# A perceiver block on one core: cross-attention's head in another order, loops written out, the context's split on another engine, and a later turn in the FFN

## The reference

```
x = x + cross_attention(layernorm(x), context)   # 16 heads of 16, 256 keys, Wq, Wk, Wv, Wo of 256 x 256, no mask
x = x + self_attention(layernorm(x))             # 16 heads of 64, causal, 64 queries
x = x + ffn(layernorm(x))                        # 256 -> 1024 -> 256, gelu; x and the hidden layer rounded to
                                                 # 16 bits by their largest magnitude, the weights to 8 bits
```

## Time and profile before

| | |
|---|---|
| the profiled execution's own time | 651.54 us |
| its span, first to last instruction | 649.7 us |
| mean granted clock of TensorE | 0.989 |
| TensorE, matmul / weight load | 602.3 us (93%) / 515.6 us (79%) |
| VectorE | 470.7 us (72%) |
| ScalarE | 386.3 us (59%) |
| GpSimd | 155.4 us (24%) |

### The profile page before, as it was taken

How to read it: one execution, slowest core, us unless ns; L and a number is a source line. 1 busy time by engine, 2 the same in 40 slices (tenths; PEclk the granted TensorE clock), 3 DMA queues, 4 the chain that set the end, 5 groups by cost and what they waited for, 6 DMA issues and landing times. The chain is left out here.

```text
span 649.7 us, 18558 instructions
## 1 busy us (share of the span) xinstructions
PE 602.3 (93%) x6777; PEld 515.6 (79%) x6777; DVE 470.7 (72%) x989; ACT 386.3 (59%) x1016; POOL 155.4 (24%) x219
## 2 busy tenths in 40 slices
PE   6599999999999999889889999999999998699997
PEld 3598888888888898758777979797979797444597
DVE  4478788888888888667899665757575657367797
ACT  3488788888888888755333333333333334257795
POOL 6524243424343423000301212112121203060000
PEclk9799999999999999999999999999999999999999
DMA  6996767676777767804000000000000000000012
GB/s 202 266 259 174 188 158 183 169 191 169 183 175 182 174 163 204 256 15 130 3 2 2 2 0 0 0 0 0 0 0 0 3 2 2 10 0 2 0 49 82
DMA packets 37036, 58.43 MB, mean 90 GB/s; under 512 B 6912, under 2 KB 15232, under 8 KB 36992
## 3 DMA queue, kind: packets, MB, share of 16 engines
q1 hardware_dynamic: 29328, 42.75, 25.7%
q10 hardware_dynamic: 4592, 8.78, 4.7%
q0 software_dynamic: 3072, 6.30, 4.0%
HBM read 17.96 MB, written 2.10 MB: 31 GB/s over the span
## 5 line engine op out<-in xcount | busy, mean ns | idle before, releaser
L617 ACT ACTIVATE Pr<-pS,nmax 128x256 f32<-128x256 f32 x256 | 120.0, 484 | 26.9 <-DVE nmax L725 26.8
L725 DVE TENSOR_REDUCE nmax<-pS 128x2 f32<-128x512 f32 x128 | 87.3, 684 | 21.7 <-PE pS L461 20.1
L471 PE MATMUL pT<-ident,Pr 128*128 128x128 f32 x512 | 78.6, 276 | 3.2 <-DVE wraw L730 3.1
L953 POOL TENSOR_TENSOR a_Pr<-a_Pr,a_rinv 128x512 f32<-128x512 f32 x32 | 32.8, 1045 | 185.8 <-DVE a_rinv L1242 185.8
L461 PE MATMUL pS<-Kst,Qst 96*128 96x256 f32 x256 | 58.9, 313 | 12.4 <-DMA Qst<-QSl 6.9
L1122 ACT ACTIVATE a_Pr<-a_Pr 128x512 f32<-128x512 f32 x32 | 20.2, 631 | 76.0 <-DVE a_Pr L1234 76.0
L471 PEld LDWEIGHTS pT<-ident,Pr 128*128 128x128 f32 x512 | 60.0, 142 | 4.5 <-issue 4.2
L461 PEld LDWEIGHTS pS<-Kst,Qst 96*128 96x128 f32 x256 | 40.3, 194 | 21.1 <-issue 9.1
L617 ACT ACTIVATION_READ_ACCUMULATOR Pr<-pS,nmax 128x1 f32 x256 | 55.1, 215 | 0.0
L280 POOL DMA_DIRECT2D Qst<-QSh x60 | 30.2, 506 | 80.8 <-PE pS L461 56.2
L59 PE MATMUL a_pJ<-a_XTh,a_W1h 128*128 128x256 f32 x128 | 37.1, 290 | 2.5 <-DVE X L1255 1.6
(11 more groups left out here) (316 smaller groups left out, 1972.9 us busy)
## 6 DMA issues: line engine op xcount, KB each, us to landing
Kst<-WO_ints SPq DMA_DIRECT2D x96, 128.0 KB, 3.3
CT<-ctxT ACTq DMA_DIRECT2D x16, 512.0 KB, 4.9
Kst<-KSh SPq DMA_DIRECT2D x62, 128.0 KB, 2.7
Qst<-QSh SPq DMA_DIRECT2D x64, 64.0 KB, 2.4
Qst<-QSh POOLq DMA_DIRECT2D x64, 64.0 KB, 3.0
Kst<-KSl SPq DMA_DIRECT2D x31, 128.0 KB, 3.2
Qst<-QSl SPq DMA_DIRECT2D x32, 64.0 KB, 2.3
Qst<-QSl POOLq DMA_DIRECT2D x32, 64.0 KB, 2.9
```

Source lines behind the costliest of these rows:

```text
L471: last = pe.transpose(pT[s % 2][:, t, k, :], Pr[s % 2][:, t, P * k:P * k + P], ident[:, :])
L617: act.activation(Pr[c % 2][:, t, :], pS[c % 2][:, t, :], ACT.Exp, bias=nmax[c % 2][:, t:t + 1], accum_out=rsum[par][:, c // 4, 2 * (c % 4) ...
L725: dve.tensor_reduce(nmax[s % 2][:, :], pS[s % 2][:, :, :], AX.X, ALU.max, negate=True).then_inc(maxed, 1)
L953: pool.tensor_tensor(rows, rows, rinv[s][:, :].unsqueeze(2).to_broadcast([P, 8, SQ]), ALU.mult).then_inc(weighted, 1)
```

## The change

**Loops.** Cross-attention and self-attention no longer have a loop: all 8 quads are written out, and the waits are by names (`made`) instead of by running numbers with a register in them.

**Events.** V of the next quad's even pair is made at steps 10 and 11 (before: 10 and 14), K of its odd pair at steps 12 and 14 (before: 11 and 12). Quad 0 has no event at steps 6 and 7.

**Head.** The order is K, X, K, Q, V, V of pair 0, K, K of pair 1, and then V, V of pair 1. The matmuls that filled TensorE's wait ahead of Q are gone. x is loaded ahead of the first weights. Of the first K, SP restacks two groups, ScalarE one and GpSimd one. Of the first Q, SP restacks one group, ScalarE one and GpSimd two, the high parts ahead of the low ones in each. On VectorE the low part of pair 1's context comes behind Q.

**Context and norm.** GpSimd now makes the high part of the context as well as the low part, and `normalize` from quad 1 on. ScalarE has the loads only, VectorE the statistics.

**FFN.** The turn stands behind slice 3 (before: 1), the split of the turned x behind slice 4 (before: 2).

The diff, cut:

```diff
-        AHEAD = [("K", 0, 0), ("K", 0, 1), ("X", 0, 0), ("Q", 0, 0), ("V", 0, 0), ("V", 0, 1), ("K", 1, 0), ("K", 1, 1)]
...
+        AHEAD = [("K", 0, 0), ("X", 0, 0), ("K", 0, 1), ("Q", 0, 0), ("V", 0, 0), ("V", 0, 1), ("K", 1, 0), ("K", 1, 1),
+                 ("V", 1, 0), ("V", 1, 1)]
...
+        def events_of(i):
+
+            p = 2 * i
+            if i == QUADS - 1:
+                return {6: ("V", p + 1, 0), 7: ("V", p + 1, 1)}
+            found = {0: ("X", p + 2, 0), 2: ("K", p + 2, 0), 3: ("K", p + 2, 1), 4: ("Q", p + 2, 0),
+                     10: ("V", p + 2, 0), 11: ("V", p + 2, 1), 12: ("K", p + 3, 0), 14: ("K", p + 3, 1)}
+            if i:
+                found.update({6: ("V", p + 1, 0), 7: ("V", p + 1, 1)})
+            return dict(sorted(found.items()))
...
-        def steps(eng, body):
-
-            body(0, False)
-            with eng.Fori(1, QUADS - 2) as i:
-                body(i, False)
-            body(QUADS - 2, False)
-            body(QUADS - 1, True)
...
+        def steps(body):
+
+            for i in range(QUADS):
+                body(i, i == QUADS - 1)
...
+        def restack_k(eng, pair):
+
+            b = pair % 2
+            eng.wait_ge(lo, made("K", pair, 1))
             apart(eng, waited)
-            after(eng, scores, chunks_done)
-            for jj in groups:
+            after(eng, scores, CHUNKS * (pair - 1))
+            for jj in range(4):
                 for u, part in enumerate((HI, HI, LO)):
...
-            restack_first_k_high(sp, (0, 1, 2))
-            restack_first_k_low(sp, (0, 1, 2))
-            restack_first_q(sp, qst_sync[0], (0, 1))
-            restack_q(sp, qst_sync[1], 1, 3, 0, (0, 1))
+            restack_first_k_high(sp, kst_in[0], (0, 1))
+            restack_first_k_low(sp, kst_in[0], (0, 1))
+            restack_first_q_high(sp, qst_sync[0], (0,))
+            restack_first_q_low(sp, qst_sync[0], (0,))
+            restack_q(sp, qst_sync[1], 1, (0, 1))
             load_x(4, 4, x_rest[1])
-            restack_k(sp, 1, 7, 0)
+            restack_k(sp, 1)
...
-                    restack_k(sp, 1, EV0 + EV * i + 8, CHUNKS * (2 * i + 2))
-                    restack_q(sp, qst_sync[1], 1, EV0 + EV * i + 3, CHUNKS * (2 * i + 2), (0, 1))
+                    restack_k(sp, 2 * i + 3)
+                    restack_q(sp, qst_sync[1], 2 * i + 3, (0, 1))
...
+            ctx_high(1)
+            restack_first_k_high(pool, kst_first, (2,))
+            restack_first_k_low(pool, kst_first, (2,))
+            restack_first_q_high(pool, qst_in[0], (2, 3))
+            restack_first_q_low(pool, qst_in[0], (2, 3))
             rstd_of(1)
-            restack_first_q(pool, qst_in[0], (2, 3))
-            restack_q(pool, qst_in[1], 1, 3, 0, (2, 3))
+            normalize(1)
+            restack_q(pool, qst_in[1], 1, (2, 3))
 
             def body(i, last):
-                if not last:
-                    ctx_low(0, 2 * i + 3)
+                if i == 0:
+                    ctx_high(2)
+                    ctx_low(2)
                 if two_ahead(i):
                     rstd_of(i + 2)
+                    normalize(i + 2)
                 if not last:
-                    restack_q(pool, qst_in[0], 0, EV0 + EV * i + 3, CHUNKS * (2 * i + 1), (2, 3))
-                    ctx_low(1, 2 * i + 4)
-                    restack_q(pool, qst_in[1], 1, EV0 + EV * i + 3, CHUNKS * (2 * i + 2), (2, 3))
...
+                    restack_q(pool, qst_in[0], 2 * i + 2, (2, 3))
+                    ctx_high(2 * i + 3)
+                    ctx_low(2 * i + 3)
+                if two_ahead(i):
+                    ctx_high(2 * i + 4)
+                    ctx_low(2 * i + 4)
+                if not last:
+                    restack_q(pool, qst_in[1], 2 * i + 3, (2, 3))
...
-                if kind == "Q":
-                    spare(5)
...
-                    if s == 8 and not last:
-                        ctx_high(1, i + 2, EV0 + EV * i + 6)
-                    if s == 15 and two_ahead(i):
-                        ctx_high(0, i + 3, EV0 + EV * i + 10)
...
+                if kind == "Q":
+                    ctx_low(1)
...
-                    if s == 8 and two_ahead(i):
-                        normalize(i + 2)
...
-                    if f == 1 and not last:
+                    if f == 3 and not last:
                         turn(g + 1)
...
-                    if f == 2 and not last:
+                    if f == 4 and not last:
                         x_high(g + 1)
...
-                    if f == 2 and not last:
+                    if f == 4 and not last:
                         x_low(g + 1)
```

More of the change, by code:

```diff
@@ L237, in ahead_bank @@
+        AHEAD_FREE = [0, 0, 0, 0, 0, 2, 1, 3, 5, 4]
         def ahead_bank(r):
             flat = [t[:, :, :, :].rearrange("p t k q -> p (t k q)") for t in pT]
[L240 to L253, removed]
@@ L255, in steps @@
-        def steps(eng, body):
-            body(0, False)
-            with eng.Fori(1, QUADS - 2) as i:
-                body(i, False)
-            body(QUADS - 2, False)
-            body(QUADS - 1, True)
-        def two_ahead(i):
[L265 to L274, removed]
+            rows = pO[:, :, :, :, :].rearrange("p g b a q -> p (g b a q)")
@@ new lines, in cross_attention, with made, event @@
+        EVENTS = [events_of(i) for i in range(QUADS)]
+        PLACE = {what: r for r, what in enumerate(AHEAD + [what for found in EVENTS for what in found.values()])}
+        def made(kind, pair, part=0):
+            return PLACE[kind, pair, part] + 1
+        def event(i, s):
+            what = EVENTS[i].get(s)
+            return what and (PLACE[what], *what)
+        def steps(body):
+            for i in range(QUADS):
+                body(i, i == QUADS - 1)
+        def two_ahead(i):
+            return i + 2 < QUADS
@@ L275, in restack_q, with k_landed, q_restacked @@
+        def k_landed(pair):
+            return RESTACK * (pair // 2 + 1) - (FIRST_BY_POOL if pair % 2 == 0 else 0)
+        def q_restacked(eng, pair):
+            eng.wait_ge(qst_sync[pair % 2], RESTACK // 2 * (pair // 2 + 1))
+            eng.wait_ge(qst_in[pair % 2], RESTACK // 2 * (pair // 2 + 1))
+        def restack_q(eng, done, pair, groups):
+            par = pair % 2
+            eng.wait_ge(lo, made("Q", pair - par))
             apart(eng, waited)
-            after(eng, scores, chunks_done)
+            after(eng, scores, CHUNKS * (pair - 1))
@@ L435, in project @@
                 elif kind == "Q":
[L436 removed]
+                    pe.wait_ge(lo, made("X", pair))
                     for g in range(2):
@@ L472, in turn, with weigh @@
                 last.then_inc(turned, 1)
[L474 to L477 removed]
+            def weigh(i, s):
+                pair, b = 2 * i + s // 8, s // 4 % 2
+                par = pair % 2
                 pe.wait_ge(pt_even, 8 * i + s // 2 + 2)
                 pe.wait_ge(pt_odd, 8 * i + s // 2 + 2)
+                pe.wait_ge(lo, made("V", pair, b))
                 if b == 0:
[L482 to L484 removed]
+                    after(pe, merged, pair)
                 for g in range(2):
@@ L518, in _ @@
             spare(10)
-            for r, (kind, ahead, part) in enumerate(AHEAD):
+            for r, (kind, pair, part) in enumerate(AHEAD):
                 if kind != "X":
                     pe.wait_ge(w_lo, W_ORDER.index("QKV".index(kind)) + 1)
-                if kind == "Q":
-                    spare(5)
-                project(r, ahead_bank(r), AHEAD_FREE[r], kind, part, ahead, ahead % 2, 3)
-            pe.wait_ge(lo, 6)
+                project(ahead_bank(r), AHEAD_FREE[r], kind, pair, part)
+            pe.wait_ge(lo, made("V", 0, 1))
             score(0, 0)
             score(0, 1)
+            pe.wait_ge(lo, made("V", 1, 1))
             pe.wait_ge(w_lo, 4)
             def body(i, last):
-                first = isinstance(i, int) and i == 0
+                first = i == 0
                 for s in range(16):
@@ L688, in _, with low @@
         def _(dve):
-            def low(r, bank, kind, ahead, part, i):
-                dve.wait_ge(hi, r + 1)
-                reused(dve, i, kind, ahead)
+            def low(bank, kind, pair, part):
+                dve.wait_ge(hi, made(kind, pair, part))
+                reused(dve, kind, pair)
                 if kind == "V":
-                    dve.tensor_copy(V[ahead % 2][:, 2 * part + 1, :], bank[:, D:2 * D]).then_inc(lo, 1)
+                    dve.tensor_copy(V[pair % 2][:, 2 * part + 1, :], bank[:, D:2 * D]).then_inc(lo, 1)
                 elif kind == "Q":
```

270 lines of the change are left out of this document (136 added, 134 removed).

## The result

The changed kernel takes 676.78 us, the median of 4 runs (674.9 to 678.5), against 651.63 of before: a ratio of 1.0387, with an interval of 1.0362 to 1.0412. The profiled execution is the run of 674.9, with a span of 673.2 us and a mean granted clock of 0.975; before they were 651.54, 649.7 and 0.989. So between the profiles 23.5 us are to be found.

A forecast was written before the change was run, and what follows sets the result against it. A quad was taken to last 22.1 us plus the time to QSh, set by SP's chain of 18 DMAs. Quads 1 to 6 +17.3, quad 7 +3.9, head -6.0, FFN -0.6: +14.6 on 651.54 gives 666.1, range 654 to 680.

The forecast's parts named there:

- The order of events: Cross-attention: K's low part 3.94 us later delays SP's 18 DMAs; quads 35.8 us, 35.4 with the context's gain.
- The score in quad 7: Quad 7 waits for the same chain: score 14.1 us after the first turn instead of 10.18, +3.9 us.
- The context's high part: Cross-attention quads: copy moved from ScalarE to GpSimd ends a TensorE wait, 0.4 us less a quad.
- If this cover were gone: Caveat on GpSimd's room for the context copies: otherwise K's projection at slot 12 waits and the chain begins later still.
- The loop written out: Cross-attention: a looped quad takes 0.65 us longer than straight quad 6; this gain is already in the 35.4.
- The self-attention: Written out too: no gain, passes keep their 32.0 us, hidden by TensorE's own work.
- The head and quad 0: Start of the kernel: Q restacked sooner and two projections leaving quad 0, -6.0 us, between nothing and 10.4.
- the two waits are for exactly the transfers that are brought forward: Head: reason for taking -6.0 us, nearer the upper end, from TensorE's 6.9 us of waits for restacked Q.
- The half clock of the earlier trace: Before, after quad 0 begins at 30.25: TensorE at half clock for 10.3 us, busy 6.97; half of that enters the 10.4.
- the 3.9 us that SP was to save with fewer DMAs: Head, first restack: SP issues 9 DMAs instead of 15, at 0.65 us each.
- The FFN: Later turn removes 1.7 us of waits, adds 1.1 of new ones: net -0.6, between -1.7 and +0.3.
- Rival B: Cross-attention: TensorE's clock falls in the new waits, 1.7 us in each of seven quads, 678 us; chance 0.15.

The follow-up runs named there:

- k_late_only: The kernel before with only the events moved: V at steps 10 and 11, the odd pair's K at 12 and 14; 676.55 us, ratio 1.0384.
- q_first: The kernel after with only SP's order turned round, restacking the odd pair's Q ahead of its K; 648.69 us, ratio 0.9951.
- k_early: The kernel after with the odd pair's K back at steps 11 and 12 and V at 10 and 14; 652.97 us, ratio 1.0023.
- pool_order: k_early, with GpSimd restacking its half of the odd pair's Q ahead of splitting the context; 645.27 us, ratio 0.9915.
- both_first: pool_order with the edit of q_first, so SP restacks the odd pair's Q ahead of its K; 643.79 us, ratio 0.9877.
- v_back: both_first, with V of pair 1 made in quad 0 again (steps 6 and 7) and not in the head; 642.87 us, ratio 0.9856.

## Why the prediction was right

*The order of events* was right in mechanism and in size. K's low part was forecast 3.94 us later and came 3.94 later; the chain was to begin 0.21 us after the first turn and did at 0.19; from there to QSh it was to take 13.9 and took 14.2 to 14.4. The quad was put at 35.4: without the 2.7 us of the clock, quads 1 to 6 take 215.19 - 2.7 = 212.5, and 6 x 35.4 is 212.4. That it fits so closely is in part luck, since two misses cancel: QSh was put at 13.7 us after the transposes, 14.1 after the turn, and came at 14.5; the rest of the quad was put at 22.1 - 0.44 - 0.4 = 21.3, and took 20.9. The score in quad 7 came 4.3 us later, forecast 3.9. `k_late_only` shows that this step alone makes the slowdown, `q_first` that it does so through SP's order.

*The context's high part* was worth more than the 0.4 us a quad: from QSh to the end 20.93 us, where quad 6 of before and the three quads of `k_late_only` without a fall of the clock have 21.67 or 21.68. But QSh comes 0.45 us later than in `k_late_only` (14.49 and 14.05 on average), and what makes that was not found. "If this cover were gone" did come true in another place: with V at step 14, GpSimd's new work pushes its half of Q into SP's chain (`k_early` against `pool_order`, some 7 us by the ratios). In the kernel after V at steps 10 and 11 keeps that away, as its timeline in quad 5 shows: the context is split from 233.95 on and the last DMA of Q goes out at 239.85, ahead of the quad at 241.75. So the order of events that suits GpSimd is the one that breaks SP's chain.

```profile
233.95 1.04 POOL L408 CAST CS0h<-CT 128x1024 fp32r<-128x1024 f32 x1 [3.54 <-issue]
...
239.85 0.50 POOL L290 DMA_DIRECT2D Qst<-QSh  x1
```

*The loop written out* was misread: 0.15 us a quad, not 0.65. The sum did not use the 0.65, since it started from quad 6, which is straight. The self-attention kept its 32.0 us a quad, as forecast.

*The head and quad 0* is the term that was wrong: -6.0, measured -1.0. The step that failed is "the two waits are for exactly the transfers that are brought forward". The half clock of the earlier trace rows was misread too: it was put behind the first turn, but the stretch begins at 25.40, 4.85 us ahead of that turn. Timelines of TensorE, before and after:

```profile
25.28 0.62 PE L461 MATMUL pS<-Kst,Qst 96*128 96x256 f32 x2 [3.55 <-DMA Qst<-QSl]
29.23 1.23 PE L461 MATMUL pS<-Kst,Qst 96*128 96x256 f32 x4 [3.33 <-DMA Qst<-QSl]
30.25 1.06 PE L471 MATMUL pT<-ident,Pr 128*128 128x128 f32 x4
```

```profile
27.07 0.71 PE L501 MATMUL pS<-Kst,Qst 96*128 96x256 f32 x4 [0.20 <-DMA Qst<-QSl]
29.54 0.77 PE L501 MATMUL pS<-Kst,Qst 96*128 96x256 f32 x2 [1.76 <-ACT Pr L649]
30.11 1.05 PE L511 MATMUL pT<-ident,Pr 128*128 128x128 f32 x4
```

GpSimd's half of Q came sooner (the second score stands at 27.38 instead of 29.23, and waits for nothing), but the half of SP and ScalarE came later, and with it the first score (27.07 instead of 25.28). Of the 3.9 us that SP was to save with fewer DMAs, 0.4 came: its last one for that score is through at 21.70 instead of 22.13, since K's restack on SP begins 1.0 us later (13.08, before 12.10) and its DMAs take longer; and it lands later. Before, the maximum and the exponentials of the first score lay in the wait for the second half; after, the first turn waits for them. That the two waits were one stretch with the softmax inside it was not seen. In quad 0 the removed projections met SP's chain for the next even pair (1.2 us of wait at 58.10, 1.66 in `both_first`), so that, by `v_back`, they are worth 0.7 us.

*The FFN*: the two waits of 1.7 us went, and three new ones for the low part of the turned X cost 0.39, 0.61 and 0.42, 1.4 in all, forecast 1.1; the fourth in the row below, 0.28 ahead of the first group, was there before with 0.20. The first layer takes 31.96 to 31.97 us in every kernel with the later turn and 32.08 to 32.17 in the three with the old one: -0.2 instead of -0.6.

```profile
PE f_bank L1543 <- DVE f_XTl L1667: 1.7, 4, 0.6
```

*Rival B* was left out of the 666 and came in part: five of the seven waits in quads 1 to 7 were followed by half clock, each at a cost of 0.35 to 1.6 us, in quad 7 1.9: 4.6 in all, where B was priced at 12. So the way from 666.0 to 676.8 is: the clock 4.6, the head 5.0, quad 7 and the FFN 0.4 each, less 1.5 for the stretch around the FFN's beginning (1.7 - 3.2), and 1.9 by which the profiled run lies under the median.

## What to carry to other kernels

Where one queue issues a row of DMAs, find the instruction that releases the first and the one that needs the last: if that chain is barely in time, a later release costs nearly its whole delay in each pass, though SP, which issues the row, has no computing to do: here 3.9 us of delay cost 3.3 us a quad. Then look at the order inside the chain before looking at its length: what was ready long before (Q here) goes out first, and the late part last. And a new job on a free engine has a place in that engine's order: what stands behind it may belong to another chain.

## What the runs showed of the hardware

After a wait of some 3 us in a busy stretch the granted clock fell to 0.50 in five of seven cases, not in all, for 3.4 or 6.8 us. The four runs of the changed kernel go by it: 674.9, 676.57, 676.99 and 678.5 us at a mean clock of 0.975, 0.972, 0.969 and 0.963. In the head, SP's last DMA for the first score was issued 0.65 us sooner (20.89 instead of 21.54) and took 6.0 us to land instead of 3.6; over the whole kernel the median of such 64 KB DMAs is 2.5. The mean DMA share until the landing is much the same, 1.06 and 1.04, so what makes this one later isn't shown. The Trainium skill (DMA: Bandwidth & Descriptors, Issuing engines are not separate DMA queues) says that starting DMAs from several engines only saves the time to initiate them, which is usually small beside the transfer. The head agrees with the first half: the half of Q that SP now shares with ScalarE landed no sooner. For a row of DMAs the second does not hold here: 12 of 128 KB take SP 7.7 to 9.2 us to issue in the rows above, and one lands 2.7 to 4.0 us after its issue in the median of the kernel after. The quads followed what stood in that row and when it began (`k_late_only`, `q_first`).
